# A cross-attention and LoRA expert kernel in float32: the prologue's work in another order on four engines

## The chip, the cores and the metric

The kernel runs on one core of a Trainium2 chip, as one launch. The metric is the device time of that launch in microseconds (us). Before the change three runs gave 297.06 us in the median, from 296.85 to 297.09.

## What is computed

The input is `x`, 32 sequences of 128 tokens with 128 features, and a context of the same shape. First comes attention with 16 heads of 8 features, without a softmax over the keys: the softmax runs over the 8 features of each head's output.

```python
q = layernorm(x) @ wq + bq;  k = ctx @ wk + bk;  v = ctx @ wv + bv      # per head
out = softmax((q @ k.T) * scale @ v, axis=-1)                          # over the 8 features
x = x + heads(out) @ wo.T + bo
```

Then a feed-forward layer with 8 experts, each a low-rank (rank 16) correction of shared weights. Two experts are chosen for each token.

```python
t = rmsnorm(layernorm(x)) * norm_w
w, chosen = top2(softmax(t @ gate_w.T))
h1 = t @ w1.T + 2 * (t @ a1[e].T) @ b1[e].T;  h3 = likewise with w3, a3, b3
act = silu(h1) * h3                                                    # 512 wide, per chosen expert
x = x + sum_e w[e] * (act @ w2.T + 2 * (act @ a2[e].T) @ b2[e].T)
```

Since there is no softmax over the keys, the kernel forms k.T @ v first ("ktv", 128 x 128 for each sequence, masked to the heads' diagonal blocks) and multiplies q by it.

## The kernel before

**Blocks.** Four sequences (512 tokens) make a block, and there are eight blocks. A step of a block is a function such as `queries(n)`; the first block's steps are split in two halves, `queries(0, 0)` and `queries(0, 1)`. Each engine has its own list of such calls, written out by hand, and the engines meet through semaphores. An engine runs its list strictly in order, so the lists' order is the schedule. For blocks 1 to 6 a loop holds the list; ahead of it stands the prologue, which is block 0 mixed with the attention of blocks 1 and 2. The change touches the prologue's lists alone: TensorE L767 to L839, ScalarE L1050 to L1110, VectorE L1467 to L1547, GpSimd L1735 to L1763, and the queue of SyncE L429 to L444.

**Splitting.** To keep precision with fast matmuls, a float32 operand is split in a rounded part ("hi") and the rest ("lo"), and a product takes three matmuls (hi x hi, lo x hi, hi x lo: `TERMS`). ScalarE writes the hi part, GpSimd or VectorE the lo part. For weights these are `weight_high` (L987) on ScalarE and `low` (L1658) on GpSimd, for five tensors in the prologue: A13, W13, B13, W2A2 and WKV. W13 and B13 arrive in the tile `act_second`, W2A2 in `v_parts`.

**Attention of a block n.** TensorE: `turn_x` (transposes the normalised x), `queries`, `keys_values` (for n = 1 `keys_values_ahead`, in two halves), `keys_times_values`, `attention_out`, `turn_heads`, `project`. Between them ScalarE evacuates (`x_turned`, `queries`, `heads_turned`) and takes the exponential `exp_o`; VectorE adds the bias to k and v (`keys_values`), masks ktv (`mask_ktv`), and makes the softmax (`top_of_o`, `shift_o`, `sum_exp`); GpSimd multiplies by the reciprocal (`norm_heads`) and makes the roots for the layer norms (`rstd_x`, `first_rstd_x1`).

**Feed-forward of block 0.** VectorE writes `tok` (`first_normalise`, L1184, a TENSOR_SCALAR from SBUF to SBUF, two instructions for each half); TensorE turns it (`turn_tok`); ScalarE and VectorE make its hi and lo parts (`tok_turned`, `tok_low`); `gate`, `top_logits` and `first_onehots` choose the experts. TensorE then runs `first_base` (the shared part of h1 and h3), `lora_in` (the rank-16 products, "u"), `first_masks` and `first_ratio`; VectorE masks u (`first_mask_u`), and `first_um_low` and `first_diff_low` make its lo parts; `hidden` adds the low-rank part to h1 and h3. `warm` (L763) fills TensorE's waits with matmuls on a constant tile.

**Banks.** PSUM has eight banks of 128 x 512. Block 1's ktv goes to `h1_ps[0]`, and its attention output to `h1_ps[1]`. `hidden_bank_free` (L610) makes the first users of `h1_ps` and `h3_ps` wait for what was there:

```python
elif b == 0 and s == 0:
    used = (ktv_done, o_shifted)[n]
    pe.wait_ge(used.sem, used.of(1))
elif b == 0:
    pe.wait_ge(kv_done.sem, kv_done.of(1, n + 1))
```

Of the kernel before, what the change touches and what calls it, by code (L numbers as in the profile page):

```python
# [41 lines left out]
AHEAD = 2  # L42
# [46 lines left out]
def build_program(nc: bass.Bass, x, ctx_t, wkv, query_w, mask_w, attn_w, rows, hidden_w, lora_w, down_w, b2, row_expert, out):  # L89
    with ExitStack() as ctx:  # L90
# [126 lines left out]
            return pair_a[i] if n == 0 else h1_ps[1] if n < AHEAD else odd_ps  # L217

        def ktv_bank(n, i):
            return pair_b[i] if n == 0 else h1_ps[0] if n < AHEAD else z_ps  # L220

        def o_bank(n, i):
            return pair_b[i] if n == 0 else h1_ps[1] if n < AHEAD else b_ps
# [177 lines left out]
        @block.sync  # L401
        def _(sp):
            def load_x(n):
                if n >= 2:
                    sp.wait_ge(x1_done.sem, x1_done.of(n - 2))
                sp.dma_start(flat(x_in[n % 2]), x[:, n * BLK:(n + 1) * BLK]).then_inc(x_loaded[n % 2].sem, 16)

            def load_ctx(n):
                if n - 1 < AHEAD:
                    sp.wait_ge(kv_mm.sem, kv_mm.of(n - 1))  # L410
                else:
                    sp.wait_ge(ctx_lo_done.sem, ctx_lo_done.of(n - 1 - AHEAD))
# [24 lines left out]
            sp.dma_start(w13_raw, hidden_w).then_inc(hidden_w_in, 16)
            sp.dma_start(b13_raw, lora_w).then_inc(lora_w_in, 16)
            load_ctx(1)
            sp.dma_start(w2a2_raw, down_w).then_inc(down_w_in, 16)  # L440
            sp.dma_start(b2_raw[:], b2).then_inc(b2_in, 16)
            load_x(2)
            load_ctx(2)
            sp.dma_start(row_expert_sb[:], row_expert).then_inc(row_expert_in, 16)  # L444
            for b in range(BLOCKS):
                if b + 3 < BLOCKS:
                    load_x(b + 3)
                    load_ctx(b + 3)
# [12 lines left out]
        def _(pe):
# [69 lines left out]

            def keys_times_values(n, i=WHOLE):
                pe.wait_ge(kv_done.sem, kv_done.of(n, upto(i)))
                if n == 1:
                    pe.wait_ge(xn_t_done.sem, xn_t_done.of(1))
                by_tile(ktv_bank(n, i), lambda t: kv[:, t, 0:P], lambda t: kv[:, t, P:2 * P], i=i)\
                    .then_inc(ktv_mm.sem, 1)

            def attention_out(n, i=WHOLE):
                pe.wait_ge(q_t_done.sem, q_t_done.of(n, upto(i)))  # L540
                pe.wait_ge(ktv_done.sem, ktv_done.of(n, upto(i)))
                by_tile(o_bank(n, i), lambda t: q_t[:, t * P:(t + 1) * P], lambda t: ktv[:, t, :], i=i)\
                    .then_inc(o_mm.sem, 1)
# [66 lines left out]
            def hidden_bank_free(b, n, s):  # L610
                free = (silu_done, act_done)[s]
                if n >= 2:
                    pe.wait_ge(free.sem, free.of(b, n - 1))
                elif b == 0 and s == 0:

                    used = (ktv_done, o_shifted)[n]
                    pe.wait_ge(used.sem, used.of(1))
                elif b == 0:
                    pe.wait_ge(kv_done.sem, kv_done.of(1, n + 1))
                elif s == 1:  # L620
                    pe.wait_ge(umf_done.sem, umf_done.of(b, 3 + n))
                else:
                    pe.wait_ge(silu_done.sem, silu_done.of(b - 1, 7 + n))
# [155 lines left out]
            warm(h1_ps[0], 6)  # L779
            attention_out(0, 1)  # L780
            keys_values_ahead(1, 0)
            warm(h1_ps[0], 16)
            turn_heads(0, 0)
            turn_heads(0, 1)
            project(0, 0)
            project(0, 1)
            keys_values_ahead(1, 1)
            turn_x(1)
            pe.wait_ge(rows_ready, 1)
            warm(h1_ps[1], 10)  # L790
# [1 line left out]
            queries(1)  # L792
            gate(0, 0)
            turn_tok(0, 1)
            keys_times_values(1)
            gate(0, 1)
            first_base(1, 1)
            lora_in(0, 0)
            lora_in(0, 1)
            first_masks(0)  # L800
            first_masks(1)
            attention_out(1)
            first_base(0, 0)
            first_ratio()
            keys_values(2, 0)
            first_base(0, 1)
            turn_x(2)
            first_base(1, 0)
            hidden(0, 0)
            hidden(0, 1)  # L810
            queries(2)
            turn_heads(1)
            keys_values(2, 1)
            project(1)
            hidden(0, 2)
# [101 lines left out]
        def _(sc):  # L917
# [134 lines left out]
            x_turned(0, 1)  # L1052
            queries(0, 0)
            weight_high(A13, attn_w_in, a13, a13_raw)
            queries(0, 1)
            exp_o(0, 0)
            exp_o(0, 1)
            weight_high(W13, hidden_w_in, w13, w13_raw)
            heads_turned(0, 0)
            heads_turned(0, 1)  # L1060
            normal_x(1)
            weight_high(B13, lora_w_in, b13, b13_raw)
            x_turned(1)
            weight_high(WKV, wkv_in, wkv_split, wkv_sb)
            tok_turned(0, 0)
            tok_turned(0, 1)
            first_spread(0, 0)
            ctx_high(2)
            first_spread(1, 0)
            queries(1)  # L1070
            first_spread(0, 1)
            first_spread(1, 1)
            first_masks(0)
            first_masks(1)
            exp_gap(0)
            normal_x(2)
            first_ratio()
            first_um_high(0, 0)
            first_um_high(0, 1)
            exp_o(1)  # L1080
            x_turned(2)
            weight_high(W2A2, down_w_in, w2a2, w2a2_raw)
            first_um_high(1, 0)
            first_um_high(1, 1)
            silu_step(0, 0)
            heads_turned(1)
            silu_step(0, 1)
# [82 lines left out]
        def _(ve):  # L1170
# [312 lines left out]
            sum_exp(0, 1)  # L1483
            round_ident()
            keys_values(1, 0)
            residual(0, 0)
            moments_x1(0, 0)
            residual(0, 1)
            moments_x1(0, 1)
            first_normalise(tok, x1[0], mv2, rstd2, rstd2_done, tok_done, 0)  # L1490
            keys_values(1, 1)
            first_normalise(tok, x1[0], mv2, rstd2, rstd2_done, tok_done, 1)
            tok_low(0, 0)
            top_logits(0, 0)
            first_onehots(0)
            tok_low(0, 1)
            top_logits(0, 1)
            moments_x(2)
            first_onehots(1)
            mask_ktv(1)  # L1500
            first_gap()
            first_mask_u(0, 0)
            first_mask_u(0, 1)
            top_of_o(1)
            first_mask_u(1, 0)
            shift_o(1)
            first_um_low(0)
            first_um_low(1)
            first_mask_u(1, 1)
            sum_exp(1)  # L1510
            first_diff_low()
# [113 lines left out]
        def _(pool):  # L1625
# [109 lines left out]
            first_rstd_x(0)  # L1735
            first_rstd_x(1)
            low(A13, a13, a13_raw)
            rstd_x(1)
            norm_heads(0, 0)
            norm_heads(0, 1)  # L1740
            low(W13, w13, w13_raw)
            first_rstd_x1(0)
            first_rstd_x1(1)
            ctx_low(2)
            rstd_x(2)
            low(WKV, wkv_split, wkv_sb)
            low(B13, b13, b13_raw)
            norm_heads(1)
            low(W2A2, w2a2, w2a2_raw)
            scale_mask(0)  # L1750
            rstd_x1(1)
            scale_step(0, 0)
# [84 lines left out]
```

## Time and profile before

| | |
|---|---|
| median of three runs | 297.06 us (296.85 to 297.09) |
| profiled execution | 298.02 us, span from the first to the last instruction 296.2 us |
| TensorE matmul busy | 287.9 us, 97% of the span, 1531 instructions |
| VectorE busy | 224.1 us, 76% |
| ScalarE busy | 187.2 us, 63% |
| GpSimd busy | 180.6 us, 61% |
| granted TensorE clock | 1.000 of full speed in the mean |

"Idle before" is the time that an engine stood still ahead of an instruction, and "releaser" is the instruction whose semaphore ended it. TensorE's matmuls overlap, so a row's duration is longer than the distance to the next row; where a stretch is gapless, the distance between two rows is what the work between them costs. A "x2" means that two instructions that follow each other are printed as one row.

### The profile page before, as it was taken

The numbers are of one execution on the slowest core, as the hardware profiler recorded it, in microseconds if no ns is written. First come the engines' busy times: TensorE is split into PE (matmuls) and PEld (weight loads), VectorE is DVE, ScalarE is ACT, GpSimd is POOL, SyncE is SP. The second block draws the span as 40 slices with busy tenths as digits, with TensorE's granted clock in tenths as the row PEclk, the third lists the DMA queues.
The fourth block names the chain that finished last, engine by engine and source line by source line (L and its number), as shares of the span: only waits on it lengthen the run. The fifth ranks groups of instructions, "written<-read, shape, count | busy, mean of one in ns | idle before, by whom it ended". The sixth has DMA issues, their size and how long they took to land. (4 is left out here: it accounts for less than half of the span.)

```text
span 296.2 us, 4607 instructions
## 1 busy us (share of the span) xinstructions
PE 287.9 (97%) x1531; PEld 240.4 (81%) x1531; DVE 224.1 (76%) x610; ACT 187.2 (63%) x310; POOL 180.6 (61%) x183
## 2 busy tenths in 40 slices
PE   8979999999999999999999999999999999999995
PEld 6757888878888888888888888888788887878884
DVE  3788986995689658894589866895579965796694
ACT  1377967674945966657755869459666558545542
POOL 3285599288980889419990589608982289518400
PEclk9999999999999999999999999999999999999999
DMA  5720020100220020200211011100012001200101
GB/s 150 287 63 10 2 71 1 74 1 8 98 74 0 0 74 35 71 3 0 71 61 49 0 41 67 71 0 2 1 37 73 0 0 38 72 1 0 38 0 35
DMA packets 7225, 12.45 MB, mean 42 GB/s; under 512 B 1825, under 2 KB 3234, under 8 KB 7202
## 3 DMA queue, kind: packets, MB, share of 16 engines
q1 hardware_dynamic: 6768, 11.77, 11.9%
q10 hardware_dynamic: 434, 0.39, 0.4%
q8 instruction: 12, 0.20, 0.3%
q14 instruction: 11, 0.09, 0.1%
HBM read 10.03 MB, written 2.13 MB: 41 GB/s over the span
## 5 line engine op out<-in xcount | busy, mean ns | idle before, releaser
L1017 ACT ACTIVATE silu<-h_ps 128x512 f32<-128x512 f32 x64 | 37.4, 596 | 33.2 <-PE h_ps L642 31.6
L1688 POOL TENSOR_TENSOR um_lo<-umf,um_hi 128x1024 fp32r<-128x1024 f32 x7 | 16.9, 2410 | 60.5 <-ACT um_hi L1009 60.5
L642 PE MATMUL h_ps<-um_hi,b_hi 128*128 128x512 f32 x128 | 51.3, 401 | 0.0
L642 PE MATMUL h_ps<-um_lo,b_hi 128*128 128x512 f32 x128 | 50.3, 393 | 0.5 <-DVE um_lo L1337 0.5
L642 PE MATMUL h_ps<-um_hi,b_lo 128*128 128x512 f32 x128 | 49.9, 390 | 0.0
L1350 DVE TENSOR_TENSOR act_second<-silu,h_ps 128x512 f32<-128x512 f32 x32 | 21.8, 680 | 17.1 <-PE h_ps L642 15.3
L1350 DVE TENSOR_TENSOR act_first<-silu,h_ps 128x512 f32<-128x512 f32 x32 | 21.4, 680 | 15.8 <-ACT silu L1017 12.7
L1710 POOL TENSOR_TENSOR scaled<-act_second,ratio 128x512 f32<-128x512 f32 x23 | 29.7, 1293 | 1.3 <-DVE act_second L1350 1.3
L642 PEld LDWEIGHTS h_ps<-um_lo,b_hi 128*128 128x128 f32 x128 | 24.0, 188 | 7.0 <-DVE um_lo L1337 1.4
L1009 ACT CAST um_hi<-umf 128x1024 fp32r<-128x1024 f32 x14 | 14.7, 1053 | 23.3 <-DVE umf L1331 22.3
L642 PEld LDWEIGHTS h_ps<-um_hi,b_lo 128*128 128x128 f32 x128 | 24.1, 188 | 4.4
L642 PEld LDWEIGHTS h_ps<-um_hi,b_hi 128*128 128x128 f32 x128 | 24.1, 188 | 4.3
L1021 ACT CAST b_hi<-act_second 128x512 fp32r<-128x512 f32 (+1 forms) x24 | 18.4, 765 | 13.7 <-DVE act_second L1350 13.7
L628 PE MATMUL h_ps<-t_hi,w_hi 128*128 128x512 f32 x64 | 26.4, 413 | 0.6 <-DVE t_lo L1252 0.6
L628 PE MATMUL h_ps<-t_hi,w_lo 128*128 128x512 f32 x64 | 25.0, 391 | 0.0
L628 PE MATMUL h_ps<-t_lo,w_hi 128*128 128x512 f32 x64 | 24.9, 390 | 0.0
L1028 ACT CAST z_hi<-act_first 128x512 fp32r<-128x512 f32 (+1 forms) x24 | 18.1, 757 | 4.4 <-DVE act_first L1364 4.1
L1725 POOL TENSOR_TENSOR z_lo<-act_first,z_hi 128x1024 fp32r<-128x1024 f32 x8 | 19.1, 2392 | 2.8 <-ACT z_hi L1028 2.8
L1410 DVE SCALAR_TENSOR_TENSOR y<-even_ps,w_first,x 128x128 f32<-128x128 f32 x28 | 7.9, 344 | 17.1 <-PE even_ps L464 17.1
L1331 DVE SCALAR_TENSOR_TENSOR umf<-h_ps,masks 128x512 f32<-128x512 f32 x28 | 17.4, 688 | 0.0
L1715 POOL TENSOR_TENSOR act_first<-act_first,scaled 128x1024 f32<-128x1024 f32 x7 | 16.7, 2382 | 0.6
L1720 POOL TENSOR_TENSOR b_lo<-act_second,b_hi 128x1024 fp32r<-128x1024 f32 x7 | 16.7, 2387 | 0.0
(296 smaller groups left out, 798.5 us busy)
## 6 DMA issues: line engine op xcount, KB each, us to landing
chosen<-choice_dram SPq DMA_DIRECT2D x7, 512.0 KB, 3.7
x_in<-in_x_dram SPq DMA_DIRECT2D x7, 256.0 KB, 2.9
ctx_in<-in_ctx_t_dram SPq DMA_DIRECT2D x7, 256.0 KB, 3.2
out_dram<-y SPq DMA_DIRECT2D x7, 256.0 KB, 2.0
act_second<-in_hidden_w_dram SPq DMA_DIRECT2D x1, 512.0 KB, 4.4
act_second<-in_lora_w_dram SPq DMA_DIRECT2D x1, 512.0 KB, 5.2
v_parts<-in_down_w_dram SPq DMA_DIRECT2D x1, 512.0 KB, 4.4
ctx_in<-in_ctx_t_dram ACTq DMA_DIRECT2D x2, 128.0 KB, 3.1
```

The costliest lines, as they stand in the source:

```text
L628: nc.tensor.matmul((h1_ps, h3_ps)[s][n % 2][:], w13[w][:, s, c * P:(c + 1) * P], t_split[b % 2][m][:], start=(i == 0), stop=False, skip_gr ...
L642: mm = nc.tensor.matmul((h1_ps, h3_ps)[s][n % 2][:], b13[w][:, s, c * P:(c + 1) * P], um[k][m][:, s, :], start=False, stop=(i == 2), skip_ ...
L1017: nc.scalar.activation(silu[:, n % SILU_RING, :], h1_ps[n % 2][:], ACT.Silu).then_inc(silu_done.sem, 1)
L1021: nc.scalar.copy(b_split[0][:, PARTS[part], :], act_second[:, PARTS[part], :]).then_inc(b_hi_done.sem, 1)
L1028: nc.scalar.copy(z_split[0][:, PARTS[part], :], act_first[:, PARTS[part], :]).then_inc(z_hi_done.sem, 1)
L1331: nc.vector.scalar_tensor_tensor(out=umf[k][:, s, :], in0=u_bank(n, s)[:], scalar=LORA_SCALE, in1=masks[n % 2][:, k, :], op0=ALU.mult, op1 ...
L1350: nc.vector.tensor_tensor((act_first, act_second)[k][:, c, :], silu[:, n % SILU_RING, :], h3_ps[n % 2][:], ALU.mult).then_inc(act_done.sem, 1)
L1688: nc.gpsimd.tensor_tensor(um[1][1][:], umf[1][:], as_f32(um[1][0][:]), ALU.subtract)\
L1710: nc.gpsimd.tensor_tensor(scaled[:, c % 2, :], act_second[:, c, :], ratio[:], ALU.mult)\
L1715: nc.gpsimd.tensor_tensor(act_first[:, 0:2, :], act_first[:, 0:2, :], scaled[:], ALU.add)\
L1720: nc.gpsimd.tensor_tensor(b_split[1][:, PARTS[0], :], act_second[:, PARTS[0], :], as_f32(b_split[0][:, PARTS[0], :]), ALU.subtract).then_i ...
L1725: nc.gpsimd.tensor_tensor(z_split[1][:, PARTS[0], :], act_first[:, PARTS[0], :], as_f32(z_split[0][:, PARTS[0], :]), ALU.subtract).then_in ...
```

## The change

Only the order of calls changes, with one bank and the waits that go with it; no instruction is added or left out.

- TensorE: block 1's second half of k and v goes ahead of the sixteen filler matmuls, its `keys_times_values` takes the place where that half stood, and its `attention_out` takes the place of `keys_times_values`. Behind `first_masks`, the order becomes both `first_base(0, .)`, `keys_values(2, 0)`, `first_ratio`, `first_base(1, 0)`, `hidden(0, 0)`, `turn_x(2)`, `hidden(0, 1)`, `turn_heads(1)`, `queries(2)`.
- ScalarE and GpSimd: W13, B13 and W2A2 are split earlier, W13 ahead of `rstd_x(1)`, W2A2 and WKV right behind `first_rstd_x1(1)` on GpSimd.
- VectorE: block 1's second k and v half and `mask_ktv(1)` come earlier, `moments_x(2)` and `first_mask_u(1, 0)` later.
- SyncE: the third context block is fetched ahead of the third x block.
- Block 1's ktv goes to `h3_ps[0]`.

```diff
-            return pair_b[i] if n == 0 else h1_ps[0] if n < AHEAD else z_ps
+            return pair_b[i] if n == 0 else h3_ps[0] if n < AHEAD else z_ps
...
-                    used = (ktv_done, o_shifted)[n]
+                    used = (xn_t_done, o_shifted)[n]
                     pe.wait_ge(used.sem, used.of(1))
                 elif b == 0:
-                    pe.wait_ge(kv_done.sem, kv_done.of(1, n + 1))
+                    used = (ktv_done, kv_done)[n]
+                    pe.wait_ge(used.sem, used.of(1))
...
             keys_values_ahead(1, 0)
+            keys_values_ahead(1, 1)
             warm(h1_ps[0], 16)
...
             project(0, 1)
-            keys_values_ahead(1, 1)
+            keys_times_values(1)
             turn_x(1)
...
             turn_tok(0, 1)
-            keys_times_values(1)
+            attention_out(1)
             gate(0, 1)
...
             first_masks(1)
-            attention_out(1)
             first_base(0, 0)
+            first_base(0, 1)
+            keys_values(2, 0)
             first_ratio()
-            keys_values(2, 0)
-            first_base(0, 1)
-            turn_x(2)
             first_base(1, 0)
             hidden(0, 0)
+            turn_x(2)
             hidden(0, 1)
+            turn_heads(1)
             queries(2)
-            turn_heads(1)
             keys_values(2, 1)
```

**GpSimd's list from the split of A13 to the context split** (`a_lo`, `w_lo`, `b_lo` from `act_second`, `w2a_lo` and `wkv_lo` are the lo parts of A13, W13, B13, W2A2 and WKV). Before:

```order
L1660 TENSOR_TENSOR a_lo<-attn_sb,a_hi 128x256
L1627 TENSOR_TENSOR neg_mean<-mv,minus_one 128x4
...
L1670 TENSOR_TENSOR heads<-e_o,rec_o 128x256 x2
L1660 TENSOR_TENSOR w_lo<-act_second,w_hi 128x1024
L1636 TENSOR_TENSOR var_eps<-mv,eps_rms 128x2
L1639 TENSOR_TENSOR rstd<-var_eps,minus_half 128x2
L1636 TENSOR_TENSOR var_eps<-mv,eps_rms 128x2
L1639 TENSOR_TENSOR rstd<-var_eps,minus_half 128x2
L1664 TENSOR_TENSOR ctx_lo<-ctx_in,ctx_hi 128x512
```

Now:

```order
L1658 TENSOR_TENSOR a_lo<-attn_sb,a_hi 128x256
L1658 TENSOR_TENSOR w_lo<-act_second,w_hi 128x1024
L1625 TENSOR_TENSOR neg_mean<-mv,minus_one 128x4
...
L1668 TENSOR_TENSOR heads<-e_o,rec_o 128x256 x2
L1658 TENSOR_TENSOR b_lo<-act_second,b_hi 128x1024
...
L1637 TENSOR_TENSOR rstd<-var_eps,minus_half 128x2
L1658 TENSOR_TENSOR w2a_lo<-v_parts,w2a_hi 128x1024
L1658 TENSOR_TENSOR wkv_lo<-wkv_sb,wkv_hi 128x256
L1662 TENSOR_TENSOR ctx_lo<-ctx_in,ctx_hi 128x512
```

W13's split now stands ahead of the root for block 1, and W2A2's and WKV's directly behind the root that the second half of `tok` needs.

**VectorE's list around `tok`.** Before:

```order
L1184 TENSOR_SCALAR tok<-x_0,mv,rstd 128x128 x2
L1203 TENSOR_TENSOR kv<-h_ps,rows_sb 128x512
L1184 TENSOR_SCALAR tok<-x_0,mv,rstd 128x128 x2
L1252 SCALAR_TENSOR_TENSOR t_lo<-even_ps,nw_sb,t_hi 128x256
L1258 COPY logits<-z_ps 128x16
```

Now:

```order
L1182 TENSOR_SCALAR tok<-x_0,mv,rstd 128x128 x2
L1210 TENSOR_TENSOR ktv<-h_ps,mask_sb 128x512
L1182 TENSOR_SCALAR tok<-x_0,mv,rstd 128x128 x2
L1250 SCALAR_TENSOR_TENSOR t_lo<-even_ps,nw_sb,t_hi 128x256
L1256 COPY logits<-z_ps 128x16
```

The k and v half between the halves of `tok` has given its place to the mask of ktv.

**TensorE's list from the end of `hidden(0, 1)` to `keys_values(2, 1)`.** Before:

```order
L642 MATMUL h_ps<-um_lo,b_hi 128x512
L529 MATMUL odd_ps<-xn_t,query_sb 128x512
L464 MATMUL even_ps<-query_sb,heads 128x128 x4
L510 MATMUL z_ps<-wkv_hi,ctx_hi 128x256
L510 MATMUL z_ps<-wkv_hi,ctx_lo 128x256
```

Now:

```order
L640 MATMUL h_ps<-um_lo,b_hi 128x512
L464 MATMUL even_ps<-query_sb,heads 128x128 x4
L529 MATMUL odd_ps<-xn_t,query_sb 128x512
L510 MATMUL z_ps<-wkv_hi,ctx_hi 128x256
L510 MATMUL z_ps<-wkv_hi,ctx_lo 128x256
```

`turn_heads(1)`, which needs GpSimd's `heads`, now stands ahead of `queries(2)`.

## Rows read from the trace of the kernel before

**Rows 1.** The table of stretches, 25 to 39 us: busy time (and instructions) by engine

```profile
core 0: us, PE busy (x) PEld busy (x) DVE busy (x) ACT busy (x) POOL busy (x), PEclk, DMA share, GB/s
25.00:39.00 14.00, 14.00 (x84) 11.43 (x85) 12.68 (x37) 11.85 (x25) 10.30 (x10) 1.00 0.01 2
```

**Rows 2.** The timeline of TensorE (PE): start, duration, instruction, [idle before <-releaser]

```profile
16.28 0.44 PE L464 MATMUL even_ps<-query_sb,heads 128*128 128x128 f32 x2 [1.15 <-POOL heads L1670]
...
24.94 0.47 PE L628 MATMUL h_ps<-t_hi,w_hi 128*128 128x512 f32 x1 [0.59 <-DVE t_lo L1252]
...
27.76 1.13 PE L469 MATMUL h_ps<-ktv,q_t 128*128 128x128 f32 x8
28.65 0.48 PE L628 MATMUL h_ps<-t_hi,w_hi 128*128 128x512 f32 x1
...
35.14 1.02 PE L529 MATMUL odd_ps<-xn_t,query_sb 128*128 128x512 f32 x2
36.00 0.60 PE L464 MATMUL even_ps<-query_sb,heads 128*128 128x128 f32 x4
...
38.19 0.48 PE L642 MATMUL h_ps<-um_hi,b_hi 128*128 128x512 f32 x1
```

**Rows 3.** The timelines of SyncE's queue and ScalarE (ACT), 6 to 31 us

```profile
6.20 0.43 SPq L437 DMA_DIRECT2D act_second<-in_hidden_w_dram  x1
...
14.92 1.03 ACT L989 CAST w_hi<-act_second 128x1024 fp32r<-128x1024 f32 x1
...
30.61 1.15 ACT L1013 CAST um_hi<-umf 128x512 fp32r<-128x512 f32 x2
```

**Rows 4.** The page's DMA issues: KB each, us from issue to landing

```profile
act_second<-in_hidden_w_dram SPq DMA_DIRECT2D x1, 512.0 KB, 4.4
```

**Rows 5.** The timeline of GpSimd (POOL), 13 to 39 us

```profile
13.80 0.20 POOL L1627 TENSOR_TENSOR neg_mean<-mv,minus_one 128x4 f32<-128x4 f32 x1 [2.66 <-DVE mv L1178]
...
16.78 2.35 POOL L1660 TENSOR_TENSOR w_lo<-act_second,w_hi 128x1024 fp32r<-128x1024 f32 x1
...
20.42 0.29 POOL L1636 TENSOR_TENSOR var_eps<-mv,eps_rms 128x2 f32<-128x2 f32 x1
20.80 0.70 POOL L1639 TENSOR_TENSOR rstd<-var_eps,minus_half 128x2 f32<-128x2 f32 x1
...
28.01 0.73 POOL L1660 TENSOR_TENSOR wkv_lo<-wkv_sb,wkv_hi 128x256 fp32r<-128x256 f32 x1
...
34.56 1.07 POOL L1670 TENSOR_TENSOR heads<-e_o,rec_o 128x512 f32<-128x512 f32 x1 [3.46 <-DVE rec_o L1234]
35.59 3.38 POOL L1660 TENSOR_TENSOR w2a_lo<-v_parts,w2a_hi 128x1024 fp32r<-128x1024 f32 x1
```

**Rows 6.** The timeline of VectorE (DVE), 20 to 37 us

```profile
20.32 0.60 DVE L1184 TENSOR_SCALAR tok<-x,mv,rstd 128x128 f32<-128x128 f32 x2
...
21.53 0.60 DVE L1184 TENSOR_SCALAR tok<-x,mv,rstd 128x128 f32<-128x128 f32 x2
22.51 0.48 DVE L1252 SCALAR_TENSOR_TENSOR t_lo<-even_ps,nw_sb,t_hi 128x256 fp32r<-128x256 f32 x1 [0.39 <-ACT t_hi L968]
...
24.20 0.48 DVE L1252 SCALAR_TENSOR_TENSOR t_lo<-odd_ps,nw_sb,t_hi 128x256 fp32r<-128x256 f32 x1
...
28.15 0.42 DVE L1316 SCALAR_TENSOR_TENSOR umf<-odd_ps,masks 128x256 f32<-128x256 f32 x1 [0.47 <-ACT masks L984]
...
33.21 0.68 DVE L1232 TENSOR_REDUCE sum_o<-e_o 128x64 f32<-128x512 f32 x1
...
34.78 1.93 DVE L1431 TENSOR_TENSOR um_lo<-umf,um_hi 128x1024 fp32r<-128x1024 f32 x1 [0.30 <-ACT um_hi L1013]
```

**Rows 7.** Instructions by line: duration in ns min/median/max, first and last start in us

```profile
L1636 POOL TENSOR_TENSOR var_eps<-mv,eps_rms x2: 194/244/293, 19.3 to 20.4; 128x2 f32<-128x2 f32 x2
...
L1308 DVE TENSOR_SCALAR den<-e_gap x8: 164/210/1333, 49.7 to 266.8; 128x4 f32<-128x4 f32 x8
...
L1337 DVE TENSOR_TENSOR um_lo<-umf,um_hi x7: 1222/1225/1226, 62.3 to 264.5; 128x1024 fp32r<-128x1024 f32 x7
```

**Rows 8.** The timeline of GpSimd at 265 us

```profile
265.74 2.40 POOL L1688 TENSOR_TENSOR um_lo<-umf,um_hi 128x1024 fp32r<-128x1024 f32 x1 [9.55 <-ACT um_hi L1009]
```

More of the change, by code:

```diff
@@ L441, in _ @@
             sp.dma_start(b2_raw[:], b2).then_inc(b2_in, 16)
+            load_ctx(2)
             load_x(2)
-            load_ctx(2)
             sp.dma_start(row_expert_sb[:], row_expert).then_inc(row_expert_in, 16)
@@ L533, in keys_times_values @@
                 pe.wait_ge(kv_done.sem, kv_done.of(n, upto(i)))
-                if n == 1:
-                    pe.wait_ge(xn_t_done.sem, xn_t_done.of(1))
                 by_tile(ktv_bank(n, i), lambda t: kv[:, t, 0:P], lambda t: kv[:, t, P:2 * P], i=i)\
@@ L1054, in _ @@
             weight_high(A13, attn_w_in, a13, a13_raw)
+            weight_high(W13, hidden_w_in, w13, w13_raw)
             queries(0, 1)
             exp_o(0, 0)
+            weight_high(B13, lora_w_in, b13, b13_raw)
             exp_o(0, 1)
-            weight_high(W13, hidden_w_in, w13, w13_raw)
+            weight_high(W2A2, down_w_in, w2a2, w2a2_raw)
             heads_turned(0, 0)
@@ L1061, in _ @@
             normal_x(1)
-            weight_high(B13, lora_w_in, b13, b13_raw)
+            weight_high(WKV, wkv_in, wkv_split, wkv_sb)
             x_turned(1)
-            weight_high(WKV, wkv_in, wkv_split, wkv_sb)
             tok_turned(0, 0)
+            queries(1)
             tok_turned(0, 1)
@@ L1069, in _ @@
             first_spread(1, 0)
-            queries(1)
             first_spread(0, 1)
@@ L1075, in _ @@
             exp_gap(0)
-            normal_x(2)
-            first_ratio()
             first_um_high(0, 0)
             first_um_high(0, 1)
+            first_ratio()
+            normal_x(2)
             exp_o(1)
-            x_turned(2)
-            weight_high(W2A2, down_w_in, w2a2, w2a2_raw)
             first_um_high(1, 0)
             first_um_high(1, 1)
+            x_turned(2)
             silu_step(0, 0)
@@ L1485, in _ @@
             keys_values(1, 0)
+            keys_values(1, 1)
             residual(0, 0)
@@ L1490, in _ @@
             first_normalise(tok, x1[0], mv2, rstd2, rstd2_done, tok_done, 0)
-            keys_values(1, 1)
+            mask_ktv(1)
             first_normalise(tok, x1[0], mv2, rstd2, rstd2_done, tok_done, 1)
@@ L1497, in _ @@
             top_logits(0, 1)
+            first_onehots(1)
             moments_x(2)
-            first_onehots(1)
-            mask_ktv(1)
             first_gap()
@@ L1504, in _ @@
             top_of_o(1)
-            first_mask_u(1, 0)
             shift_o(1)
@@ L1508, in _ @@
             first_um_low(1)
+            first_mask_u(1, 0)
             first_mask_u(1, 1)
@@ L1737, in _ @@
             low(A13, a13, a13_raw)
+            low(W13, w13, w13_raw)
             rstd_x(1)
@@ L1740, in _ @@
             norm_heads(0, 1)
-            low(W13, w13, w13_raw)
+            low(B13, b13, b13_raw)
             first_rstd_x1(0)
             first_rstd_x1(1)
+            low(W2A2, w2a2, w2a2_raw)
+            low(WKV, wkv_split, wkv_sb)
             ctx_low(2)
             rstd_x(2)
-            low(WKV, wkv_split, wkv_sb)
-            low(B13, b13, b13_raw)
             norm_heads(1)
-            low(W2A2, w2a2, w2a2_raw)
             scale_mask(0)
```

## The prediction

> **What bounds the kernel now.** I read the table of stretches first: from 25 to 39 us TensorE is busy 14.00 of 14.00 us [rows 1]. Then its timeline, to see where that begins: it waits 1.15 us for GpSimd's first heads at 16.28, and its last wait of note ends at 24.94, where `first_base(1, 1)` starts on VectorE's t_lo [rows 2]. Call that start S. From S to `hidden(0, 2)` at 38.19 TensorE needs 13.25 us without a gap [rows 2], and what follows is TensorE's own work. So a change to the prologue counts by two sums: how far it moves S, and how much longer or shorter than 13.25 us the way from S to `hidden(0, 2)` gets. I take the rest to move along unchanged. Both ways lead through VectorE and GpSimd [rows 5, 6]; last I looked for rows in which these two hold each other up [rows 5 to 8].
>
> **The gain that the order offers.** Block 1's second k and v half moves into a place where TensorE filled and idled ahead of 16.28, ktv takes its place, and attention_out(1) takes ktv's. So attention_out(1), 28.65 - 27.76 = 0.89 us [rows 2], leaves the gapless stretch. In its new place TensorE waited for t_lo anyway. That 0.89 us is all there is to gain; `turn_x(2)` only moves within the stretch.
>
> **W13 ahead of the root, +0.2 us on S.** W13's data land 4.4 us after 6.20, at 10.6 [rows 3, 4]; the cast takes 1.03 [rows 3], GpSimd's part 2.35 [rows 5]: 13.98. The chain of `rstd_x(1)`, behind it in GpSimd's order, started at 13.80 [rows 5] and leads without a pause to the heads for which TensorE waits at 16.28 [rows 2]. So S moves by some 0.2 us. Below, nothing if the data land sooner; above, 0.4 us with semaphores between. B13 takes the place that W13 had, in front of the same wait, and costs nothing.
>
> **W2A2 and WKV behind the root, +2.3 us on S.** GpSimd's `rstd` for the second half of `tok` ends at 20.80 + 0.70 = 21.50, and VectorE starts `tok` at 21.53 [rows 5, 6]. Now GpSimd goes on at that moment with W2A2's lo part, 2.35 us, so both start within some hundredths of a microsecond.
>
> What the rows show of such a meeting: a TENSOR_SCALAR from SBUF to SBUF, `den`, takes 164 ns alone, and 1333 ns at 266.8, where it ends as GpSimd's um_lo does, 265.74 + 2.40 = 268.14 [rows 7, 8]. The other way round, GpSimd's var_eps took 293 in place of 194 ns when it met the first half of `tok`: 0.10 us, so it slipped in between that half's two instructions [rows 5 to 7]. And at 34.78 VectorE's um_lo, 1.22 us elsewhere, took 1.93 while GpSimd's heads ran to 35.63, then GpSimd's w2a_lo took 3.38 in place of 2.35 [rows 5 to 7]. So `tok` is of a kind that shares something with GpSimd, and whoever holds it keeps the other out to the end of an instruction.
>
> The Trainium skill, "SBUF — State Buffer", section "Who interferes with whom", says that VectorE and GpSimd share a pair of ports as an exclusive lock for a whole instruction, and names tensor_scalar and two-input operations from SBUF among those that take it. By that rule `tok` waits, as in my sum; by the 0.10 us of the var_eps row alone it would hardly be touched, and the sum would be the first rival's below.
>
> I take the full wait, by the `den` row, which is nearest in kind. GpSimd, moved by 0.2, runs W2A2 from 21.7 to 24.05. Then the first `tok` instruction runs, wkv_lo (0.73 [rows 5]) slips in as var_eps did, and the second follows (each half of `tok` takes 0.60 [rows 6]): done at about 25.0, where it was 22.13. From there VectorE has work without a pause: t_lo of the first half to t_lo of the second is 24.20 - 22.51 = 1.69 [rows 6], and from that to S 24.94 - 24.20 = 0.74 [rows 2, 6]. S becomes 25.0 + 1.69 + 0.74 = 27.4, that is +2.5 with the 0.2. If VectorE wins the start, or wkv_lo comes last, about 0.5 us less. Nothing lies beside this: TensorE has nothing left but gate, ktv and fillers, all shorter.
>
> **From S to `hidden(0, 2)`, +1.55 us in place of -0.89.** Order now: `turn_heads(1)` ahead of `queries(2)`. In the trace heads(1) ended at 34.56 + 1.07 = 35.63, `queries(2)` ran from 35.14 to 36.00, and so covered that wait [rows 2, 5]. When would heads(1) be there now? Its chain starts with the masks of u at 28.15, S + 3.21 [rows 2, 6], behind the same TensorE work as before. From there VectorE does the same instructions in another order to sum_exp(1) at 33.21, 5.06 us [rows 6]; GpSimd starts heads 34.56 - 33.21 = 1.35 later and needs 1.07 [rows 5, 6]. Sum: S + 10.69. I take VectorE as the later of the two engines here; should ScalarE's exponential come later, all shifts by it. TensorE's own work ahead of it took 35.14 - 24.94 = 10.2 us [rows 2] and is now 0.89 us shorter, so without other waits TensorE stands at `turn_heads(1)` at S + 9.3 and waits: heads(1) decide.
>
> Then a second meeting. `first_diff_low` (two inputs from SBUF, 1.22 us [rows 7]) stands right behind sum_exp(1) on VectorE. Before, it waited for ScalarE until 34.78, after heads had begun [rows 5, 6]. Now ScalarE's um_high(1, .), two in 1.15 us [rows 3], come directly behind the exponential, and end before VectorE's sum and reciprocal (1.35 with the semaphore). So first_diff_low starts at once, a little before heads, and heads wait for most of its 1.22 us: about 1.05. Bounds: 0 if heads start first, 1.2.
>
> So turn_heads(1) starts at S + 10.69 + 1.05 = S + 11.75. Behind it come `queries(2)`, 36.00 - 35.14 = 0.86, and the same rest as before, 38.19 - 36.00 = 2.19 [rows 2]: `hidden(0, 2)` at S + 14.8, against S + 13.25. That is +1.55; without the second meeting +0.5. The 0.89 us is lost inside this wait either way.
>
> **At nothing.** The context fetch ahead of x(2) and the bank change: the data are needed only behind the second half of the prologue, and the new waits are on work long done. W2A2's old place, 3.38 us of GpSimd [rows 5], goes free, but TensorE has no gap there to close [rows 1].
>
> **Sum.** 2.5 + 1.55 = +4.05 us. The profiled execution took 298.02 us, 0.96 over the median of the runs; a difference carries over, so 297.06 + 4.05 = 301.1 us.
>
> **Rivals.**
> 1. *`tok` does not wait for GpSimd.* For it: only `den` shows a full wait, and that one has no per-partition scalars; the var_eps row shows 0.10 us. Against it: um_lo and heads waited for each other to the end. S moves by 0.2, heads(1) decides as above: +0.2 + 0.5 = +0.7 (297.8), or +1.75 with the second meeting (298.8).
> 2. *Only the first meeting.* Heads win over first_diff_low, or um_high is late: 2.5 + 0.5 = +3.0 (300.1); with VectorE first at `tok`, 299.5. For it: the starts lie within 0.1 to 0.2 us.
> 3. *The order pays: faster.* If there is no meeting at `tok` and heads(1) are ready when TensorE gets there, the full 0.89 us less 0.2 is kept: 296.4. The point from which it decides: heads(1) must end by S + 9.3 (10.2 - 0.89), 1.4 us sooner than my sum of VectorE's row distances. For it: VectorE's pauses ahead of 28.15 (0.47 us idle [rows 6]) could let the masks start sooner. Against it: these wait for TensorE's u and mask products, which have not moved against S.
> 4. *The end absorbs it.* Later stages have slack on the other engines, TensorE none [rows 1]; a late start could be made up only in TensorE's later waits, which I count as too few: no change.
>
> **Numbers.** A difference of 0.2% (0.6 us) is about what a measurement can tell from none. Both meetings, in their variants (300.5 to 301.7): 0.48. The first alone (299.4 to 300.3): 0.26. Rival 1: 0.13, of which 0.08 near 298.8. Rival 3: 0.08. No change: 0.05. The range from 298.5 to 301.7 leaves out rival 3, no change, and the lower half of rival 1, together 0.18. Slower by over 0.2%: 0.48 + 0.26 + 0.11 of rival 1 = 0.85, since its lower end lies close to that bound; same 0.05 + 0.01 = 0.06; faster 0.08 + 0.01 = 0.09.
>
> **What would show it.** In the profile after: a `tok` row of over 2 us in VectorE's timeline, ending with GpSimd's w2a_lo or wkv_lo; TensorE idle for over 2 us ahead of `turn_tok(0, 1)`; `first_base(1, 1)` near 27.4; TensorE idle for 1 to 2 us ahead of turn_heads(1), released by heads; and a heads row of some 2 us beside first_diff_low. If `tok` takes 0.6 us as before, the main term is wrong. If TensorE reaches `hidden(0, 2)` at or before 38.19, the prediction is wrong in sign.

## The result and the profile after

The changed kernel takes 303.5 us in the median of six runs (301.88 to 303.99), the kernel before 297.24 us beside it (296.85 to 297.44). The ratio is 1.0188, 95% interval 1.0170 to 1.0207; it is an estimate of its own, and the quotient of these two medians, 1.021, lies just above that interval. Slower was forecast, but 301.1 us, and the range ended at 301.7. So the sign held and the size did not.

| | before | after |
|---|---|---|
| profiled execution / its span | 298.02 / 296.2 us | 302.54 / 300.7 us |
| granted clock in the mean | 1.000 | 0.994; 0.987 to 0.994 in the six runs |
| S, start of `first_base(1, 1)` | 24.94 | 27.34 |
| `hidden(0, 2)` | 38.19 | 42.47 |

Columns of a timeline are, as in [rows 2]: start, duration, engine, line, operation, tiles, count, and in brackets the idle time ahead and its releaser. VectorE's timeline of the kernel after has the two instructions that the prediction named:

```profile
20.37 0.60 DVE L1182 TENSOR_SCALAR tok<-x,mv,rstd 128x128 f32<-128x128 f32 x2
21.57 3.04 DVE L1182 TENSOR_SCALAR tok<-x,mv,rstd 128x128 f32<-128x128 f32 x2
...
36.99 0.55 DVE L1232 RECIPROCAL rec_o<-sum_o 128x64 f32<-128x64 f32 x1
37.46 1.16 DVE L1429 TENSOR_TENSOR um_lo<-umf,um_hi 128x1024 fp32r<-128x1024 f32 x1
```

GpSimd's timeline of the same execution has their partners:

```profile
13.93 0.25 POOL L1625 TENSOR_TENSOR neg_mean<-mv,minus_one 128x4 f32<-128x4 f32 x1
...
15.65 1.22 POOL L1668 TENSOR_TENSOR heads<-e_o,rec_o 128x256 f32<-128x256 f32 x2
...
21.51 2.34 POOL L1658 TENSOR_TENSOR w2a_lo<-v_parts,w2a_hi 128x1024 fp32r<-128x1024 f32 x1
23.81 0.72 POOL L1658 TENSOR_TENSOR wkv_lo<-wkv_sb,wkv_hi 128x256 fp32r<-128x256 f32 x1
...
37.62 1.92 POOL L1668 TENSOR_TENSOR heads<-e_o,rec_o 128x512 f32<-128x512 f32 x1 [5.73 <-DVE rec_o L1232]
```

Both meetings took place. The second half of `tok` took 3.04 us where it took 0.60 [rows 6], beside w2a_lo and wkv_lo. Later heads(1) took 1.92 where it took 1.07 [rows 5]; the 0.85 more are spent beside a first_diff_low that kept its own 1.16. TensorE's timeline shows what this does to it:

```profile
24.76 0.41 PE L464 MATMUL odd_ps<-query_sb,tok 128*128 128x128 f32 x2 [1.94 <-DVE tok L1182]
25.01 1.83 PE L469 MATMUL h_ps<-ktv,q_t 128*128 128x128 f32 x8
26.63 0.86 PE L469 MATMUL b_ps<-attn_sb,tok_t 128*128 128x8 f32 x4
27.34 0.77 PE L626 MATMUL h_ps<-t_hi,w_hi 128*128 128x512 f32 x1
27.92 0.63 PE L626 MATMUL h_ps<-t_lo,w_hi 128*128 128x512 f32 x1
...
39.60 0.66 PE L464 MATMUL even_ps<-query_sb,heads 128*128 128x128 f32 x4 [1.47 <-POOL heads L1668]
...
42.47 0.48 PE L640 MATMUL h_ps<-um_hi,b_hi 128*128 128x512 f32 x1
```

Behind the wait of 1.94 us TensorE's own rows are longer than before: attention_out(1), the eight matmuls from ktv, takes 1.83 where it took 1.13, and the first matmul of `first_base(1, 1)` 0.77 where it took 0.47 [rows 2]. The table of stretches says why (columns as in [rows 1]; the third value from the end is the granted clock):

```profile
24.00:25.00 1.00, 0.24 (x2) 0.27 (x3) 1.00 (x3) 0.00 (x0) 0.53 (x1) 1.00 0.00 0
25.00:26.00 1.00, 1.00 (x8) 1.00 (x7) 0.89 (x11) 0.73 (x2) 0.00 (x0) 0.55 0.00 0
26.00:27.00 1.00, 1.00 (x7) 1.00 (x6) 0.66 (x3) 1.00 (x4) 0.00 (x0) 0.50 0.00 0
27.00:28.00 1.00, 1.00 (x5) 0.90 (x5) 0.41 (x4) 0.32 (x2) 0.90 (x1) 0.50 0.00 0
28.00:29.00 1.00, 1.00 (x5) 0.81 (x4) 0.92 (x8) 0.28 (x1) 0.37 (x1) 0.75 0.00 0
29.00:30.00 1.00, 1.00 (x6) 0.65 (x4) 0.96 (x9) 0.42 (x2) 0.00 (x0) 1.00 0.00 0
```

TensorE is busy throughout from 25 on and gets 0.50, the lower of its two levels (1.2 GHz), until past 28. In the prediction this does not occur. In the trace of the kernel before every one of these stretches has 1.00 [rows 1].

### The profile page after: what moved, and what is told of

It is laid out like the page before. It is cut to its first block and busy times, and to the rows that moved or that the text cites. A ratio compares the mean times of both kernels' runs of the same rounds, so it can differ in the third digit from the quotient of the medians.

```text
span 300.7 us, 4606 instructions
## 1 busy us (share of the span) xinstructions
PE 288.7 (96%) x1531; PEld 241.5 (80%) x1531; DVE 226.9 (75%) x610; ACT 188.0 (63%) x310; POOL 180.3 (60%) x183
```

## The experiments

The first theory after the result: the two meetings are as forecast, and what is missing is the granted clock behind the wait for `tok`. The rival: the meetings, the order or W13 cost more than I gave them. Each time is the median of a run's own executions less that of the kernel before on the same chip, with the interval of the ratio behind it.

**a1_fill.** The kernel after, with 32 fillers in the wait for `tok`.

```diff
+            warm(h1_ps[0], 32)
             turn_tok(0, 1)
```

> The changed kernel with 32 filler matmuls ahead of turn_tok(0, 1), where TensorE waits 1.94 us for tok. The clock theory (the wait for tok is long enough that TensorE's granted clock falls to half, 0.50 to 0.55 from 25 to 28 us): the clock stays at 1.00 through 25 to 30 us, gate(0, 1) and first_base(1, 1) run at full speed, lora_in starts 1.0 us sooner than 28.66, and the time falls from 303.5 to between 301.0 and 302.5 us with less spread between runs. The port theory alone (GpSimd's W2A2 part keeps tok out) expects tok still at 3.0 us, and no change of the time: 303.5 us.

Measured: 301.92 against 297.86, +4.06 (1.0126 to 1.0157). Its mean clock is 0.998 to 1.0. TensorE's timeline:

```profile
22.32 1.95 PE L763 MATMUL h_ps<-scrap 128*128 128x128 bf16 x32
24.41 0.41 PE L464 MATMUL odd_ps<-query_sb,tok 128*128 128x128 f32 x2
24.66 1.06 PE L469 MATMUL h_ps<-ktv,q_t 128*128 128x128 f32 x8
...
26.60 0.47 PE L626 MATMUL h_ps<-t_hi,w_hi 128*128 128x512 f32 x1 [0.48 <-DVE t_lo L1251]
```

Its table of stretches:

```profile
25.00:28.00 3.00, 2.52 (x17) 2.25 (x16) 2.78 (x19) 1.98 (x5) 1.25 (x1) 1.00 0.00 0
```

`tok` is held as long as ever (3.05 us from 21.21), the clock stays at 1.00, and the work behind the wait is back at 1.06 and 0.47. The intervals of after and a1 do not touch: 1.0188 - 1.0142 of 297.9 us is 1.4 us for the clock, and by the two differences of medians (6.26 and 4.06) it is 2.2. It may be more: a1's executions spend 1.9 to 2.5 us outside the span from the first to the last instruction, all others 1.7 to 1.9, and by the spans alone a1 costs 3.55 us (299.65 against 296.10), which leaves 2.7 for the clock. What that extra time of a1 is, no run shows.

**a2_w2late.** The kernel after, with W2A2 and WKV off `tok`.

```diff
-            low(W2A2, w2a2, w2a2_raw)
-            low(WKV, wkv_split, wkv_sb)
             ctx_low(2)
             rstd_x(2)
+            low(WKV, wkv_split, wkv_sb)
             norm_heads(1)
+            low(W2A2, w2a2, w2a2_raw)
```

> The changed kernel with GpSimd's lo parts of W2A2 and WKV back where they stood before, behind ctx_low(2) and rstd_x(2); ScalarE's casts stay early. Port theory: tok takes 0.6 us again, first_base(1, 1) starts near 25.0, TensorE has no wait for tok and the clock stays at 1.00; heads of block 1 still wait for first_diff_low (1.9 us in place of 1.07), so hidden(0, 2) starts 14.9 us behind first_base(1, 1), near 39.9: 297.2 + 1.7 = 298.9 us. If the loss came from the order on TensorE alone, it stays near 303 us.

Measured: 300.69 against 297.86, +2.83 (1.0080 to 1.0110), so 1.1 over what I expected. `tok` takes 0.60 and S is 24.89, but TensorE has a new wait further on:

```profile
30.41 0.39 PE L510 MATMUL b_ps<-wkv_hi,ctx_hi 128*128 128x256 f32 x1 [1.29 <-POOL wkv_lo L1658]
...
37.88 0.66 PE L464 MATMUL even_ps<-query_sb,heads 128*128 128x128 f32 x4 [1.71 <-POOL heads L1668]
```

The change moves `moments_x(2)` back on VectorE, so `rstd_x(2)` is late on GpSimd, and WKV's split behind it too. The first meeting is gone; a queue on GpSimd behind a late root took part of its place.

**a3_swap.** The kernel after, with `queries(2)` ahead of `turn_heads(1)` as before.

> The changed kernel with queries(2) ahead of turn_heads(1) again, as before. Order theory: the wait of 1.47 us ahead of turn_heads(1) is covered in part, hidden(0, 2) starts 0.86 us sooner, and the time is 302.6 us; if the runs that lost more clock lost it in this second wait, up to 1 us more, 301.6 us. Theory that only the first meeting counts: no change, 303.5 us.

Measured: 302.81 against 297.86, +4.95 (1.0148 to 1.0180). TensorE waits 0.61 for heads in place of 1.47, as expected, but its profiled execution had the clock at 0.50 from 24 to 30, longer than after's. The 0.7 us to after's ratio (1.3 by the differences of medians) lies inside the scatter that the clock makes, and the two intervals overlap, so no gain is shown.

**b1_weights.** The kernel before, with the change's weight splits alone, on ScalarE and GpSimd.

> The kernel before with the weights' split moved alone (ScalarE's casts and GpSimd's lo parts in the order of the change), TensorE and VectorE as before. Port and clock theory: tok takes 3 us, first_base(1, 1) starts 2.0 us later or more, heads of block 1 meet first_diff_low and cost another 0.5 us behind queries(2), and the clock falls for some us (1 to 2 us): 300.7 to 301.7 us. If the loss lies in the order on TensorE, the time stays at 297.2 us.

Measured: 301.40 against 297.86, +3.54 (1.0110 to 1.0144). S is 27.38. The clock fell here too, at another place: 0.91 in 17 to 18, then 0.50 to 21, behind a wait of 1.33 us for heads(0) at 16.47; behind the 1.30 us for `tok` it stayed at 1.00.

**b2_order.** The other half: the kernel after with all weights split where before split them. Two details: W13's cast on ScalarE stands one place earlier than in before, here and in b4, d1 and d2 (it fills a gap: in b4 it runs from 12.57 to 13.60, and the exponential behind it still waits 0.69 us for VectorE). And this half holds moves on ScalarE that the list of the change does not name: `queries(1)` forward, `normal_x(2)` and the ratio behind the first um_high.

> The other half of the change alone: the kernel after with all five weights' high and low parts back at the places that ScalarE and GpSimd had before; the new order on TensorE, VectorE, the queue SP and the rest of ScalarE stays. My theory (the weights' order alone cost 3.54 us; the order costs by another mechanism): tok takes 0.60 again and S is near 24.9, but WKV's low part stands behind rstd_x(2), which now waits for the later moments_x(2), so keys_values(2,0) waits some 1.3 us for wkv_lo, and heads is held by um_lo (1.9): +2.5 to +3.2 on before, 300.4 to 301.1, the clock at 1.0. Rival 1, the order pays by itself (the earlier attention moves 0.9 us of work out of the stretch): 0.5 to 0.9 under before, 297.0 to 297.4. Rival 2, the order changes nothing: within 0.3 of before. If it is over +1.5, the two halves do not add up to the whole (+5.6), since they share the meetings.

Measured: 300.51 against 297.44, +3.07 (1.0095 to 1.0126). Rivals 1 and 2 of that text are out: the order by itself costs. TensorE's timeline has three of its waits:

```profile
14.04 2.80 PE L491 MATMUL h_ps<-wkv_sb,ctx_in 128*128 128x256 f32 x8 [1.72 <-DMA ctx_in<-in_ctx_t_dram]
...
32.48 0.39 PE L510 MATMUL b_ps<-wkv_hi,ctx_hi 128*128 128x256 f32 x1 [1.28 <-POOL wkv_lo L1658]
...
40.48 0.66 PE L464 MATMUL even_ps<-query_sb,heads 128*128 128x128 f32 x4 [1.49 <-POOL heads L1668]
```

The first belongs to this execution, which took 303.13, the longest of five: the transfer of block 1's context took 5.6 us from issue to landing (at most 3.5 in before), TensorE had reached its first reader by 12.4, and the clock was 0.50 from 15 to 18 behind the wait. That reader, `keys_values_ahead(1, 0)`, stands where it stood before. The other two waits are those of a2.

**c1_nomeet1.** The kernel after, with GpSimd's order `ctx_low(2)`, WKV, `rstd_x(2)`, `norm_heads(1)`, W2A2.

> The kernel after with GpSimd's order ctx_low(2), WKV, rstd_x(2), norm_heads(1), W2A2: neither low part beside the second tok, and WKV in time. My theory: the first meeting is gone without the new wait of the run a2; tok takes 0.60, S is near 24.9, keys_values(2,0) waits for nothing, the second meeting stays (heads 1.9 beside um_lo, TensorE waits for it 1 to 1.7), the clock stays at 1.0: hidden(0,2) begins near 39.4 (38.19 in before), so +1.0 to +1.7 on before, about 1.3 below a2. Rival, the first meeting and the clock behind it were not what a2 removed, and WKV's wait in a2 cost nothing: as a2, +2.8. Second rival, the order pays once the first meeting is gone: under before by 0.3 to 0.9.

Measured: 299.64 against 297.44, +2.20 (1.0063 to 1.0104), over the expected 1.0 to 1.7. S is 25.12 and WKV is in time. Left are, in TensorE's timeline:

```profile
31.37 0.47 PE L626 MATMUL h_ps<-t_hi,w_hi 128*128 128x512 f32 x1 [0.59 <-DVE e_o L1225]
...
36.98 0.66 PE L464 MATMUL even_ps<-query_sb,heads 128*128 128x128 f32 x4 [1.46 <-POOL heads L1668]
```

The starts of these executions differ. In before's execution VectorE's first `top_o` began at 11.64, in c1's at 10.79 and in after's at 10.65; yet heads(0) came at 15.60, 15.74 and 15.65. The early start was lost in between, and W13's split stands there.

**b3_w13.** The kernel before with W13 alone moved as in the change.

```diff
             weight_high(A13, attn_w_in, a13, a13_raw)
+            weight_high(W13, hidden_w_in, w13, w13_raw)
...
             low(A13, a13, a13_raw)
+            low(W13, w13, w13_raw)
             rstd_x(1)
```

> The kernel before with one weight moved as in the change: W13's high part ahead of queries(0,1) on ScalarE, its low part ahead of rstd_x(1) and heads(0) on GpSimd; all else as before. In the traces the first top_o of block 0 begins at 10.6 us in some runs and at 11.6 in others, and with W13 ahead heads(0) is at 15.6 in both, so the early start is lost. My theory now: W13 costs nothing in a late start and up to 1.0 in an early one (wo_sb takes 1.07 beside w_lo, neg_mean waits for w_lo): heads(0) is not before 15.6, +0.3 to +1.0 on before. Rival, W13 costs at most the 0.2 of my prediction: within 0.2 of before. Rival, it frees GpSimd behind heads(0) and pays: under before.

Measured: 298.26 (12 runs) against 297.55 (23 runs), +0.71 (1.0004 to 1.0038, that is 0.1 to 1.1 us). VectorE's and GpSimd's timelines:

```profile
10.88 0.42 DVE L1219 TENSOR_REDUCE top_o<-z_ps 128x32 f32<-128x256 f32 x1 [0.18 <-PE z_ps L469]
...
13.18 1.00 DVE L1422 SCALAR_TENSOR_TENSOR wo_sb<-rows_sb,attn_sb 128x128 f32<-128x128 f32 x1
```

```profile
11.69 2.35 POOL L1660 TENSOR_TENSOR w_lo<-act_second,w_hi 128x1024 fp32r<-128x1024 f32 x1 [0.99 <-ACT w_hi L989]
14.00 0.25 POOL L1627 TENSOR_TENSOR neg_mean<-mv,minus_one 128x4 f32<-128x4 f32 x1
...
15.72 1.22 POOL L1670 TENSOR_TENSOR heads<-e_o,rec_o 128x256 f32<-128x256 f32 x2
```

From `top_o` to heads(0) pass 3.96 to 3.97 us in the six traces in which w_lo stands behind heads(0) (before, b2, b4, d1, d2, e2), and up to 5.13 in the eight in which it stands ahead; most with the early starts. W13 holds the root back, and a meeting that I had not looked for holds VectorE back: `wo_sb` took 0.28 us in before's trace, here 1.00, until w_lo had ended at 14.04.

**b4_w2kv.** The kernel before with W2A2's and WKV's low parts behind the second root (W2A2's high part early on ScalarE), W13 (but for its cast, see b2) and B13 as before.

> The kernel before with the low parts of W2A2 and WKV behind the second root on GpSimd, as in the change, and W2A2's high part early on ScalarE; W13 and B13 behind heads(0) and rstd_x(2) as before, TensorE and VectorE untouched. It prices the first meeting by itself. My theory: the second tok is held until wkv_lo is done, S near 27.4, the granted clock falls for 2 to 4 us behind that wait, W2A2's low part is no longer beside um_lo of step 1 (which may give 0.3 back): +2.4 to +3.2 on before, so that it and W13 (0.7) make up the weights' +3.5. Rival, tok is not the matter and W13 or B13 made up most of the weights' cost: under +1.5.

Measured: 301.87 against 297.32, +4.55 (1.0111 to 1.0161), far over the expected 2.4 to 3.2. The meeting is as expected (`tok` 3.04 us, TensorE's wait 1.94, S 27.28). The clock fell for longer than I allowed, as in a3:

```profile
23.00:24.00 1.00, 0.00 (x0) 0.00 (x0) 1.00 (x2) 0.00 (x0) 1.00 (x2) 0.74 0.00 0
24.00:25.00 1.00, 0.59 (x3) 0.62 (x4) 0.96 (x6) 0.00 (x0) 0.18 (x1) 0.50 0.00 0
...
29.00:30.00 1.00, 1.00 (x4) 0.71 (x4) 0.93 (x10) 0.31 (x2) 0.74 (x3) 0.50 0.00 0
30.00:31.00 1.00, 1.00 (x7) 0.67 (x6) 0.54 (x2) 0.40 (x2) 0.92 (x3) 0.85 0.00 0
```

Its runs at mean clocks of 0.991 to 0.993 took 300.6 to 302.3 us, those at 0.988 302.4 and 302.6. That this part costs more than all weights in b1 is not shown, since the two intervals overlap; in b1 the clock fell elsewhere.

**c2_nomeet12.** c1 with the second meeting taken away too, by orders on three engines:

```diff
             first_ratio()
+            exp_o(1)
             normal_x(2)
-            exp_o(1)
+            x_turned(2)
             first_um_high(1, 0)
             first_um_high(1, 1)
-            x_turned(2)
...
+            sum_exp(1)
             first_mask_u(1, 0)
             first_mask_u(1, 1)
-            sum_exp(1)
...
-            hidden(0, 1)
+            queries(2)
             turn_heads(1)
-            queries(2)
+            hidden(0, 1)
```

> c1 and the second meeting taken away: on ScalarE exp_o(1) and normal_x(2), x_turned(2) ahead of first_um_high(1,0), with exp_o(1) ahead of normal_x(2); on VectorE sum_exp(1) ahead of first_mask_u(1,0); on TensorE queries(2) and turn_heads(1) ahead of hidden(0,1). My theory: sum_exp starts near 32.1 and heads near 33.4 with no um_lo beside it, so it takes 1.07; turn_heads starts near 34.5, hidden(0,1) near 35.0 to 35.5, hidden(0,2) near 37.9: -0.3 on before, range -0.9 to +0.6 (the difference of block 0, step 1 comes later, and hidden(0,1) may wait 0.5 for it). Rival, heads is held by something else than the um_lo beside it: heads takes 1.9 still, and the time stays at c1's +1.0 to +1.7.

Measured: 299.12 against 297.44, +1.68 (1.0046 to 1.0072), not the -0.9 to +0.6 expected. heads(1) takes 1.07 again, at 33.66, but TensorE now waits 0.77 for a mask of u ahead of `queries(2)` at 34.97. On VectorE a third meeting stands: the one-hots of the second half, 0.26 us in after, take 0.95 at 25.70 beside GpSimd's ctx_lo (25.24, 1.29 us). Before had the statistics of `moments_x(2)` at that place. The one-hots take as long in a1 (0.93) and a2 (0.96).

**e2_w13_moments.** c2 with W13's and B13's low parts and `moments_x(2)` back where before has them.

> The kernel c2 (both meetings gone, +1.68) with W13's and B13's low parts back behind heads(0) and rstd_x(2) and moments_x(2) back ahead of first_onehots(1) on VectorE, so that the statistics and not the one-hots (0.28 alone, 0.95 in c2) lie beside ctx_lo. My theory: what c2 still lost is W13 (0.3 to 1.0) and this third meeting with the later statistics (0.3), so +0.2 to +1.0 on before, and heads(0) again follows the start. Rival, the rest of c2's loss lies in the order behind first_masks (queries(2) waits for umf, the table load behind um_hi): c2's +1.5 to +1.8 stays.

Measured: 299.30 against 297.55, +1.75 (1.0043 to 1.0074). My theory fails, and the time is the rival's. TensorE's waits lie around and behind `first_masks`: 0.28 for a spread, 0.40 for e_o and 0.77 for xn_t:

```profile
27.55 0.50 PE L585 MATMUL b_ps<-ident_bf,spread 128*128 128x128 bf16 x4 [0.28 <-ACT spread L978]
...
31.11 0.47 PE L626 MATMUL h_ps<-t_hi,w_hi 128*128 128x512 f32 x1 [0.40 <-DVE e_o L1225]
...
34.94 1.10 PE L529 MATMUL odd_ps<-xn_t,query_sb 128*128 128x512 f32 x2 [0.77 <-ACT xn_t L934]
```

One suspect was taken away only in part: the one-hots still took 0.61, now beside wkv_lo.

**d1_early_o.** What the order can give at best: the early k, v and attention of the change, the weights (but W2A2's early high part, and W13's cast, see b2) as before, the rest of TensorE's and ScalarE's order as before (but for `first_base(0, 1)` and block 1's `queries(1)`, which stay early), and on VectorE:

```diff
             first_gap()
+            top_of_o(1)
+            shift_o(1)
             first_mask_u(0, 0)
             first_mask_u(0, 1)
-            top_of_o(1)
             first_mask_u(1, 0)
-            shift_o(1)
+            first_mask_u(1, 1)
             first_um_low(0)
             first_um_low(1)
-            first_mask_u(1, 1)
             sum_exp(1)
```

> A version meant to keep what the order offers: the change's early k, v and attention of block 1 on TensorE (the second half of k, v behind the fillers), its context queue, W2A2's high part early on ScalarE; GpSimd's list, W13, B13, WKV and moments_x(2) as before; behind that the order of before on TensorE and ScalarE, and on VectorE top_o(1), shift_o(1) ahead of the first mask_u, and the first diff_low as before. My theory: attention_out(1) fits into the wait for t_lo (0.59 in before) and S stays near 24.9, the 0.89 of attention goes out of the stretch behind it, and heads is ready by 34.7 without a meeting, so hidden(0,2) begins at 37.3 to 37.7 (38.19): -0.9 to -0.3 on before. Rival, VectorE's and ScalarE's chain of umf, um_hi, um_lo bounds that stretch as much as TensorE does, so the attention only moves TensorE's idle time: within 0.3 of before.

Measured: 297.69 (11 runs) against 297.55 (23 runs), +0.14 (0.9999 to 1.0027): the rival holds. From S, 24.74, to `hidden(0, 2)`, 37.87, are 13.13 us in place of 13.25. The 0.89 us of attention are out of this stretch. TensorE gives them back, all but 0.1: in two waits of its weight loads (PEld), for ScalarE and for VectorE, and some 0.1 us at the masks:

```profile
30.56 0.42 PEld L464 LDWEIGHTS z_ps<-query_sb,xn 128*128 128x128 f32 x4 [0.30 <-ACT ratio L996]
...
32.41 0.19 PEld L640 LDWEIGHTS h_ps<-um_lo,b_hi 128*128 128x128 f32 x1 [0.44 <-DVE um_lo L1320]
```

**d2_um_first.** d1 with um_hi and the ratio ahead of `normal_x(2)` on ScalarE, and `turn_x(2)` between `hidden(0, 0)` and `hidden(0, 1)` on TensorE.

> d1 (+0.14) with two moves: on ScalarE the two um_hi of block 0 and the ratio ahead of normal_x(2), on TensorE turn_x(2) between hidden(0,0) and hidden(0,1). In d1 TensorE's loads waited 0.30 for the ratio and 0.44 for um_lo, behind a ScalarE without a gap. My theory: that chain was what gave the attention's 0.89 back, so hidden(0,0) starts near 31.1 (31.8 for its first um_hi), hidden(0,2) near 37.2 to 37.5: -0.7 to -0.2 on before. Rival: other waits of the same chain take their place (um_lo behind B13's low part on GpSimd, xn late for queries(2)), and it stays within 0.3 of before or goes over it.

Measured: 298.87 against 297.32, +1.55 (1.0033 to 1.0061). Again the rival: TensorE waits 0.42 for um_lo, the exponential comes later, and heads_t is 0.71 us late for `project(1)`. ScalarE's um_hi was done by 30.38 here, yet um_lo began at 30.97: VectorE was busy with its eight masks of u until then. So the wait for um_lo is set by VectorE's order as well as by ScalarE's. No version that beats the kernel before was found.

## Why the prediction was wrong

**What held.** Both meetings were there, at the instructions named, with `tok` at 3.04 us and heads at 1.92; S was 27.34 against 27.4, though 0.38 us of that is the clock (from the start of `tok` to S pass 5.77 us in after, 5.39 in a1); TensorE waited 1.94 us for `tok` (over 2 was forecast) and 1.47 for heads, and the 0.89 us of the order were lost. a1 is the kernel of the forecast, without the clock, and cost +4.06 where the sum was +4.05. That the two agree so closely is partly luck: its terms were off and cancelled, and by the spans a1 cost 3.55.

- *W13, "+0.2 us on S", was mis-sized.* By itself it cost 0.71 (b3; the interval reaches down to 0.1). I compared 13.98 with the 13.80 of one execution, which had started late (`top_o` at 11.64); in executions that start 1 us sooner the root could run 1 us sooner, and W13 takes that away. I also missed that `wo_sb` meets w_lo.
- *The first meeting, "+2.3 us on S".* Measured from the start of `tok` to S: 24.94 - 21.53 = 3.41 before [rows 2, 6]; in a1 `tok` began at 21.21, so 26.60 - 21.21 = 5.39, +1.98, between the forecast 2.3 and its lower variant, some 0.5 less.
- *S to `hidden(0, 2)`, "+1.55".* In a1 41.16 - 26.60 = 14.56, +1.31. A wait that the sum lacks, 0.74 us for e_o ahead of `first_base(1, 0)` in after and a1, cost nothing here, since it lies ahead of the longer wait for heads. With W13 the three make 0.71 + 1.98 + 1.31 = 4.00.

**The step that failed.** "TensorE has nothing left but gate, ktv and fillers, all shorter" (by the list of the change it is attention_out(1), not ktv): I priced its wait by the waiting alone, and all behind it at the rates of before. The sum has no term for the clock that TensorE is granted. In the trace of before the wait of 1.15 us at 16.28 [rows 2] had left it at 1.00, and I took that for granted. It fell behind the 1.94 us and cost 1.4 to 2.2 us (after against a1; 2.7 by the spans). One trace was too few to take it for granted: of the 23 runs of the kernel before beside b3 two have a mean clock of 0.994, and they took 299.32 and 299.69 us where the median is 297.55. In after the clock also spread the runs: 301.88 and 302.54 at a mean clock of 0.994, 303.46 and 303.55 at 0.989, 303.78 and 303.99 at 0.987. The profiled execution, 302.54, is one of the two shortest, and against a1's it shows only 0.95 us for the clock (0.38 up to S, 0.57 from S to `hidden(0, 2)`). That hid the size of the miss in its trace, where `hidden(0, 2)` at 42.47 is close to the forecast of 42.2.

**The rivals.** `tok` did wait (against rival 1), heads did not win (2), nothing was absorbed (4). Rival 3, the order pays, does not fail at the heads alone, as I had it: in d1 they are ready in time, and the gain is still gone. As I read the traces, the cause is that ScalarE is without a gap from 27.33 to 34.89 in d1 (masks, xn, ratio, um_hi, the exponential, a table load), VectorE has none up to 33.5, and TensorE needs the results of both on the way; no run took this limit away and showed the gain. By the split of the change, the weights alone cost 3.54 and the order alone 3.07; that these nearly add up to 6.26 is no proof that the causes add, since the order alone waits 1.28 us for wkv_lo and the whole change does not.

**The meetings.** The rows of `tok` (3.04 for 0.60), wo_sb (1.00 for 0.28), heads (1.92 for 1.07) and the one-hots (0.95 for 0.26) show one of VectorE and GpSimd held for most of the other's instruction. The Trainium skill, "SBUF — State Buffer", section "Who interferes with whom", describes a lock between the two that is held for a whole instruction; the traces agree.

**What stays open.** Why the clock fell behind some waits and not behind others of like length, and for how long it stays low, was not tried. What c2 lost in all is not settled either; its waits are named, but e2 took away one suspect and part of another and gained nothing. What TensorE waits for in d1 and d2 was not taken away either.

## What to carry to other kernels

A weight split moved into another engine's idle time is free only if no work of VectorE on the path of a kind that met here (`tok`, wo_sb, the one-hots, um_lo) stands beside it, and no root stands behind it; look at what runs on the *neighbour* there. A wait that a change adds on TensorE costs more than its length if the clock falls behind it: 32 fillers in it won 1.4 us or more here. Taking work out of a gapless engine gained nothing here (d1) while the engines that feed it were as good as gapless over the same stretch, so read their timelines before counting the gain.

## What was not expected of the hardware

- The granted clock went to 0.50 behind TensorE's waits of 1.94 us (after, a3, b4), 1.72 (b2) and 1.33 (b1), but not behind 1.46 (a1, c1), 1.71 (a2) or 1.27 (b3). The length of the last wait does not by itself tell. In a3 and b4 the rows have it low before TensorE starts again (0.50 in 24 to 25, 0.74 in 23 to 24).
- The first steps start up to 1 us earlier or later: VectorE's first `top_o` lay between 10.58 (b2) and 11.64 us (before, c2), and c1 and c2, whose lists are the same up to there, have 10.79 and 11.64. Each kernel has one trace, so an edit in the first 16 us must be read against that.
